# The order of two VectorE instructions in an attention stage: low part and running maximum

## The reference

```
scores = einsum('blhd,bmhd->bhlm', q * 36**-0.5, k)
attn   = softmax(scores)                 # over m, 1024 long
o      = einsum('bhlm,bmhd->blhd', attn, v)
```

## Time and profile before

| what | value |
|---|---|
| median of 3 runs | 3302.26 us (3299.76 to 3304.22) |
| the profiled execution | 3293.01 us, span 3291.3 us |
| busy share of the span | PE 88%, PEld 70%, DVE 52%, ACT 43%, POOL 46% |
| mean granted TensorE clock | 0.937 of full |
| attention stage | about 718 to 1889 us of the span |
| busy in 780 to 1860 us | PE 1024.8, DVE 899.6, ACT 964.9, POOL 901.5 of 1080 us |

### The profile page before, as it was taken

One profiled execution on the slowest core, in us unless ns is written; L12 is line 12 of the kernel. 1 busy time (PEld: TensorE's weight loads), 2 busy tenths in 40 slices (PEclk: granted clock), 3 DMA queues, 4 the chain that ended last, 5 costly groups with the idle time before them and its releaser, 6 DMA issues. The chain is left out here.

```text
span 3291.3 us, 49525 instructions
## 1 busy us (share of the span) xinstructions
PE 2889.1 (88%) x16066; PEld 2291.0 (70%) x16066; DVE 1710.2 (52%) x2926; ACT 1399.2 (43%) x1758; POOL 1524.9 (46%) x1144
## 2 busy tenths in 40 slices
PE   6759899967999999999999867649999999999976
PEld 2247777844666666666666556549999999999965
DVE  3446566546888888888888667831111111111125
ACT  2112222215888888898888812211111111111112
POOL 1232322115888888888888848842222222222210
PEclk9869899977999999999999978869999999999988
DMA  5365566561333333333333157567121121111144
GB/s 168 135 228 203 184 212 216 187 176 42 73 80 78 70 80 81 71 76 81 75 73 80 39 175 243 209 225 230 35 69 35 35 69 35 48 56 35 49 138 145
DMA packets 337308, 373.72 MB, mean 114 GB/s; under 512 B 166161, under 2 KB 229273, under 8 KB 337166
## 3 DMA queue, kind: packets, MB, share of 16 engines
q1 hardware_dynamic: 329688, 359.12, 36.7%
q10 hardware_dynamic: 7482, 12.69, 1.3%
HBM read 221.81 MB, written 149.36 MB: 113 GB/s over the span
## 5 line engine op out<-in xcount | busy, mean ns | idle before, releaser
L757 POOL TENSOR_TENSOR a_pl<-a_pf,a_ph 128x1024 fp32r<-128x1024 f32 x384 | 913.1, 2398 | 57.0 <-ACT a_pf L840 56.6
L774 DVE TENSOR_REDUCE a_mx<-a_psum_s 128x1 f32<-128x1024 f32 x512 | 626.0, 1223 | 203.2 <-PE a_psum_s L855 195.1
L838 ACT ACTIVATE a_ph<-a_psum_t 128x1024 fp32r<-128x1024 f32 x512 | 526.1, 1027 | 166.6 <-PE a_psum_t L870 148.0
L1424 POOL TENSOR_TENSOR m_al<-m_af,m_ah 128x256 fp32r<-128x256 f32 x288 | 212.5, 738 | 764.9 <-DVE m_ah L1433 764.9
L1472 PE MATMUL m_psum_h<-m_ht,m_w 128*128 128x256 f32 x4032 | 533.3, 283 | 33.6 <-DMA m_w<-w_s 25.0
L1472 PEld LDWEIGHTS m_psum_h<-m_ht,m_w 128*128 128x128 f32 x4032 | 507.4, 189 | 37.2 <-issue 37.1
L1433 DVE CAST m_ah<-m_af 128x256 fp32r<-128x256 f32 x288 | 84.6, 294 | 837.0 <-ACT m_af L1410 837.0
L1486 PE MATMUL m_psum_y<-m_w,m_ah 128*128 128x288 f32 x2304 | 504.4, 296 | 1.4 <-DVE m_y L1450 1.2
L1410 ACT ACTIVATE m_af<-m_psum_h,m_bias 128x256 f32<-128x256 f32 x288 | 137.3, 477 | 813.4 <-PE m_psum_h L1472 813.4
L887 PE MATMUL a_psum_o<-a_ph,a_vs 128*100 128x512 f32 x1024 | 406.6, 397 | 3.7 <-POOL a_pl L757 3.6
L888 PE MATMUL a_psum_o<-a_pl,a_vs 128*100 128x512 f32 x1024 | 403.9, 394 | 0.0
(11 more groups left out here) (215 smaller groups left out, 3184.8 us busy)
## 6 DMA issues: line engine op xcount, KB each, us to landing
a_qs<-q_s SPq DMA_DIRECT2D x192, 144.0 KB
a_ks<-k_s SPq DMA_DIRECT2D x192, 144.0 KB
w_s<-q_ws SPq DMA_DIRECT2D x64, 324.0 KB, 3.4
h_s<-p_ht SPq DMA_DIRECT2D x40, 512.0 KB, 5.3
m_ht<-h_s SPq DMA_DIRECT2D x16, 1280.0 KB, 8.1
v_s<-q_vo SPq DMA_DIRECT2D x64, 288.0 KB, 2.3
a_vs<-v_s SPq DMA_DIRECT2D x128, 144.0 KB
q_s<-q_qko SPq DMA_DIRECT2D x32, 512.0 KB, 2.7
```

The source lines that it names most:

```text
L757: pool.tensor_tensor(pl[:, s % RING], pf[:, s % RING], raw(ph[:, s % RING]), ALU.subtract).then_inc(lo_pool, 1)
L774: dve.tensor_reduce(mx[:, u % 2, t:t + 1], p_s[:], AX.X, ALU.max).then_inc(s_free, 1)
L838: act.activation(ph[:, s % RING], p_t[:, s % 2], ACT.Exp, scale=SCALE)
L1424: pool.tensor_tensor(al[:, f % RING], af[:, f % RING], raw(ah[:, f % RING]), ALU.subtract).then_inc(lo_ready, 1)
```

## The change

In steps k = 2 and k = 6 of VectorE's loop, the call of `low` is moved ahead of the call of `max_tile` (and of `turn`, which is only in k = 8, a step without `low`). Each instruction keeps its own waits. Nothing is added or removed, and the other engines' programs are the same. The instructions ahead of the loop keep their order.

```diff
                     for k in range(1, STEPS + 1):
                         over, s = divmod(k, STEPS)
+                        if s + LO_AHEAD in DVE_LO and not (last and u + over == SLOTS):
+                            low(hd + over, s + LO_AHEAD)
+                        if s + LO_AHEAD - STEPS in DVE_LO and not (last and u == SLOTS - 1):
+                            low(hd + 1, s + LO_AHEAD - STEPS)
                         if not (last and u + over >= SLOTS - 2):
                             max_tile(hd + over + 2, (u + over + 2) % SLOTS, s)
                         if over and not (last and u >= SLOTS - 2):
                             turn(hd + 2, (u + 2) % SLOTS, i + 1)
-                        if s + LO_AHEAD in DVE_LO and not (last and u + over == SLOTS):
-                            low(hd + over, s + LO_AHEAD)
-                        if s + LO_AHEAD - STEPS in DVE_LO and not (last and u == SLOTS - 1):
-                            low(hd + 1, s + LO_AHEAD - STEPS)
                         if (s + 1) % PER_LH == 0:
                             finish_hi(hd, s // PER_LH)
```

## The result

The changed kernel takes 3443.09 us (median of 5 runs, 3441.34 to 3444.17), the kernel before 3301.31 us (median of 5, 3295.14 to 3304.22). The ratio is 1.0433, with a 95% interval of 1.0418 to 1.0447: 142 us slower. The forecast was 3441, and +139.

The account below looks back on a forecast made before the run. The attention was taken as bound by the score tile and maximum loop through p_s. Low parts 131.4 us plus loop rounds 7.7 gave 139; 3302.3 + 139 = 3441 us, range 3424 to 3462.

Parts of the forecast that it names:

- The loop of score tile and maximum bounds the stage, with no slack: In attention, PE's score tile and DVE's maximum wait for each other through p_s, 2.06 us a bare step.
- The low part can't start before its exponential, 0.38 behind the maximum's data: On DVE, the moved low part waits for ScalarE's second exponential, starting 0.38 us later than the maximum could have.
- The maximum then waits 1.13 for DVE: On DVE, the low part holds the engine 1.13 us from its start until a ready maximum can start.
- PE's wait for the low part is gone, with 0.46 in return: On PE, scores' 0.40 us buffer wait vanishes; the 2.28 and 2.29 us steps become 2.06 again.
- Each low part +1.06: Four attention steps around each low part take 9.76 instead of 8.70 us; 124 low parts give 131.4 us.
- Rounds of the loop, 7.7 us: At 14 round starts, ScalarE's table load delays the low part 0.55 us more than now, 7.7 us in all.
- The clock stays at 1.00: PE, 85% busy in the attention after the change, keeps its full 2.4 GHz clock, judged by profile rows.
- The second rival: PE's clock swings to half: 3612 us with one slow step behind each stall, 3929 if all slow; 5%.
- The row of a 2.05 us gap at full clock: Evidence from the MLP: PE 5.95 of 8 us busy with a 2.05 us gap, clock still 1.00.
- the 9.3 us from the profiled time to the median: Added to the profiled 3293.0 us to reach the median 3302.3, the base for the forecast of 3441.
- The cover for GpSimd: POOL's low parts keep enough room in the longer head; without this cover, 12 us more.
- ready in time: Exponential finishes early, low part fits DVE's gap, starting by T5 + 2.15 (T5: step 5's score tile release); 3265 us, 3%.

Follow-up runs that it names:

- e5: Changed kernel, but in the two low-part steps ScalarE's second activation covers 512 of 1024 columns and goes to SBUF; ratio 1.0261 to the kernel before.
- e6: Changed kernel, but VectorE's low part covers only 512 of 1024 columns, the rest of its buffers zeroed once; ratio 1.0234 to the kernel before.
- e4: Kernel before, with TensorE in steps 0 and 4 running values' high products, then scores, then the low products; 3268.74 us, ratio 0.9916.
- e2: Changed kernel with only the low part of step 1 (k = 6) ahead of its maximum; ratio 1.0278 to the kernel before.
- e7: Changed kernel plus TensorE's split values (high products, scores, low products in steps 0 and 4); ratio 1.0533 to the kernel before.
- e1: Changed kernel with only the low part of step 5 (k = 2) ahead of its maximum; ratio 1.0183 to the kernel before.
- e3: Changed kernel with the 14 low parts that meet ScalarE's table load put back behind their maximum; ratio 1.0326 to the kernel before.
- e9: Old VectorE order with split values, head loop as 5 rounds of 12 heads instead of 15 of 4; ratio 0.9961 to the kernel before.
- e8: Changed kernel with the head loop as 5 rounds of 12 heads instead of 15 of 4; ratio 1.0475 to the kernel before.

## Why the prediction was right, step by step

1. *The loop of score tile and maximum bounds the stage, with no slack.* Right. After, the bare steps are 2.04 to 2.06 as before, and what is lost in one step is never won back.
2. *The low part can't start before its exponential, 0.38 behind the maximum's data.* Right: 1504.78 against 1504.42 for a maximum (0.77 behind its tile), 0.36. e5 shows the chain: the exponential ends 0.45 earlier and the whole interval shrinks by 0.43.
3. *The maximum then waits 1.13 for DVE.* Right, 1.14; e6 takes half of it away and gets 0.54 back.
4. *PE's wait for the low part is gone, with 0.46 in return.* Right in the sum. PE's stall for the maximum in its place is about 1.1 us behind the low part of step 5 and 1.45 behind that of step 1, where I said 1.4 for all. e4 showed that these 0.46 are two parts, which the prediction did not separate.
5. *Each low part +1.06.* It was +1.02: the interval is 9.72, not 9.76. I took 2.06 for the bare steps where the trace had 2.05 for most of them. 124 x 0.04 = 5 us too much.
6. *Rounds of the loop, 7.7 us.* Measured: (10.70 - 9.72) - (9.10 - 8.70) = 0.58, 14 x 0.58 = 8.1.
7. *The clock stays at 1.00.* Wrong at 7 places of 124. The second rival was given 5% as a thing that happens behind each stall or not at all. It happened behind half of the long ones only, which are at the rounds. Seven falls at 1.15 to 1.36 us cost 8.7. I had the length of that stall in my hands (an ordinary 1.4 and 0.97 more at the rounds) and asked about the clock for the ordinary one alone. The row of a 2.05 us gap at full clock was no bound for one of 2.4, and by e5 and e6 not even for gaps of its own length: 2.0 and 1.9 us brought falls there.

The sum: 126.5 + 8.1 + 8.7 = 143.3 against 131.4 + 7.7 = 139. The terms off by 5 and by 9 nearly cancel, so the 2 us of distance flatter the working; 4 us of 142 is what it is worth. There is luck in the 9.3 us from the profiled time to the median as well: the profiled execution after was itself the median, 3443.09, 11 above the 3432 that the forecast had for it, of which 8.9 are the later start of the attention. The cover for GpSimd held: from 800 to 1800 us PE waited 0.3 us for its low parts in all.

The rival "ready in time" named its own point of decision, a low part that starts by T5 + 2.15. It starts at T5 + 3.2 in every ordinary interval. The Trainium skill's rule of a clock that swings with waits for PSUM ("TensorE: Matmul & The Clock Gate", "A second HAM failure mode: psum-queue depth-cycling") speaks of short idles that come often. It did not hold here: behind the 110 ordinary stalls of up to 1.5 us, each a wait for the PSUM buffer of the score tile, the clock stayed at 2.4 GHz. The falls came behind single longer stalls, one a round.

## What to carry to other kernels

Before moving an instruction ahead of another on an in-order engine, put the time at which each one's data are ready side by side: whoever is put first lends its wait to the other. If the one put behind is in the loop that sets the pace, the loss is what its data are ready later (0.37 us here) and the whole run time of the first (1.13), and the saved wait of a third engine pays back only what it cost (0.46 of 1.5 us here). Where a consumer waits in line for such a value, look first for work of its own that it can do meanwhile: e4 moves two products and gains 28 us where the reordering lost 142. And look at the irregular places, the rounds of a loop, by themselves; stalls add up there.

## What the runs showed of the hardware that I had not expected

- One long stall of PE in a dense stream was enough for a fall of the clock to 1.2 GHz, but not each time. Of the 14 rounds in a profiled execution it fell in 6 behind 1.9 us (e6), in 5 behind 2.0 (e5), in 7 behind 2.4 (the changed kernel), and in 13 behind 2.55 (e2 and e7). Behind the stalls of up to 1.5 us in e1 and e3, 62 and 110 in a run, it stayed at 2.4 GHz; so it did behind a gap of 2.05 us in the MLP. What decides between equal stalls is open.
- A fall cost the stage 1.15 to 1.36 us in the changed kernel, and up to 2.5 in e7, where the clock stayed low for about twice as long.
- The turn of a hardware loop got dearer with a larger body. On the old order with split values, 4 heads a round cost 0.66 us a turn (e4), 12 heads 2.9 to 6.4 (e9). On the new order, 4 heads cost 1.0, and 1.2 to 1.4 more where the clock fell; 12 heads cost 9.4 to 11.8 with 10 to 14 us at 1.2 GHz in it (e8). Only these two sizes were run, and what the time goes into is not shown.
